# Attention scores as four column tiles of 32 keys with staged queries, in a two-layer conv, scan, attention and expert kernel

## What is computed

```python
qkv = jnp.einsum('bnc,ce->bne', x, W_qkv)          # B=4, N=4096, C=128
q, k, v = jnp.split(qkv, 3, axis=-1)               # HEADS=4, DIM_HEAD=32
q = l2norm_axis1(q); k = l2norm_axis1(k)           # over the tokens
sim = jnp.einsum('bihd,bjhd->bhij', q, k) * SCALE
attn = jax.nn.softmax(sim, axis=-1)
out = jnp.einsum('bhij,bjhd->bhid', attn, v)
```

## Time and profile before

| | |
|---|---|
| three runs | 6005.42, 6006.07, 6010.80 us; median 6006.07 |
| profiled execution | 5990.85 us, its span 5989.1 us |
| TensorE matmul busy | 4802.9 us (80%) |
| VectorE busy | 5104.7 us (85%) |
| ScalarE busy | 3730.3 us (62%) |
| attention loops | four stretches; the first begins at 822 us and its last exponential starts at 1384 us |

### The profile page before, as it was taken

How to read it: one execution, slowest core, us unless ns; L and a number is a source line. 1 busy time by engine, 2 the same in 40 slices (tenths; PEclk the granted TensorE clock), 3 DMA queues, 4 the chain that set the end, 5 groups by cost and what they waited for, 6 DMA issues and landing times. The chain is left out here.

```text
span 5989.1 us, 76415 instructions
## 1 busy us (share of the span) xinstructions
PE 4802.9 (80%) x21528; PEld 1760.4 (29%) x21592; DVE 5104.7 (85%) x6562; ACT 3730.3 (62%) x4769; POOL 1754.4 (29%) x1306
## 2 busy tenths in 40 slices
PE   5767779998666777999867677799986767789997
PEld 2222422223322242222332224222233222422223
DVE  6799779998779977999868996799987899679998
ACT  1666368883266636888326663788832666378882
POOL 3488500000148850000014885000001588400000
PEclk8899989999889998999988999899988899989998
DMA  1000020000000002000000000200000000020000
GB/s 38 0 1 0 15 54 0 0 0 22 22 0 1 0 15 54 0 0 0 22 22 0 1 0 15 54 0 0 0 22 22 0 1 0 15 54 0 0 0 15
DMA packets 26646, 69.25 MB, mean 12 GB/s; under 512 B 11224, under 2 KB 13088, under 8 KB 23328
## 3 DMA queue, kind: packets, MB, share of 16 engines
q1 hardware_dynamic: 26400, 66.43, 4.4%
HBM read 26.55 MB, written 8.39 MB: 6 GB/s over the span
## 5 line engine op out<-in xcount | busy, mean ns | idle before, releaser
L1257 ACT ACTIVATE arena<-ps 128x1024 f32<-128x1024 f32 x2048 | 1982.8, 1024 | 282.7 <-PE ps L1228 242.0
L1272 DVE TENSOR_TENSOR arena<-arena 128x1024 f32<-128x1024 f32 x1664 | 1913.9, 1220 | 130.3 <-ACT arena L1257 130.2
L916 DVE TENSOR_TENSOR_SCAN arena<-ps,hlast,arena 128x512 f32<-128x512 f32 x1024 | 1267.3, 1281 | 5.2 <-DVE arena L898 3.2
L876 POOL TENSOR_TENSOR arena<-arena 128x1024 f32<-128x1024 f32 x512 | 1206.9, 2357 | 22.6
L1228 PE MATMUL ps<-arena 128*128 (+1 forms) x4096 | 1079.8, 384 | 87.5 <-issue 61.6
L1212 PE MATMUL ps<-arena 128*32 128x512 f32 x8192 | 1077.0, 603 | 38.2 <-DVE arena L1277 35.2
L845 ACT ACTIVATE ps<-arena,amat 128x512 f32<-128x512 f32 x1024 | 692.0, 688 | 508.2 <-DVE arena L916 507.5
L813 PE MATMUL ps<-arena,ident 128*128 128x512 f32 x2048 | 970.2, 597 | 7.7 <-POOL arena L876 7.7
L1572 POOL MEMSET arena<- 128x1024 f32 x4 | 3.8, 956 | 2771.8 <-POOLq L101 2771.8
L1228 PEld LDWEIGHTS ps<-arena 128*128 128x128 f16 x4096 | 316.1, 98 | 1194.6 <-ACT arena L1257 807.1
L898 DVE TENSOR_TENSOR arena<-arena,ps 128x1024 f32<-128x1024 f32 x512 | 618.4, 1208 | 45.2 <-remote 30.9
(11 more groups left out here) (242 smaller groups left out, 4402.5 us busy)
## 6 DMA issues: line engine op xcount, KB each, us to landing
arena<-x SPq DMA_DIRECT2D x32, 512.0 KB, 5.9
arena<-arena SPq DMA_DIRECT2D x64, 256.0 KB, 6.0
arena<-arena SPq DMA_DIRECT2D x64, 224.0 KB, 5.8
arena<-pe SPq DMA_DIRECT2D x256, 32.0 KB, 1.8
out<-arena SPq DMA_DIRECT2D x8, 1024.0 KB, 3.9
expw<-L_ffn_expert_w SPq DMA_DIRECT2D x1, 512.0 KB
wqkv<-L_attn_W_qkv SPq DMA_DIRECT2D x1, 192.0 KB
wx<-in_projT SPq DMA_DIRECT2D x1, 128.0 KB
```

The source lines that it names most:

```text
L876: pool.tensor_tensor(halves(g[s % 4]), halves(hb[s % 4]), cs[s % 4].unsqueeze(1).broadcast_to([128, HD, CH]), ALU.mult).then_inc(hc_s, 1)
L916: dve.tensor_tensor_scan(halves(hb[s % 4])[:, h, :], da(s, h), halves(dbx[s % 2])[:, h, :], k.hlast[:, s, h, :], ALU.mult, ALU.add).then_i ...
L1257: act.activation(probs[p % 8], k.bank(2 * group[p], 2 * CH), ACT.Exp, scale=SCALE / SPLIT ** 2).then_inc(exp_s, 1)
L1272: dve.tensor_tensor(acc[p % 2], acc[p % 2], probs[p % 8], ALU.add).then_inc(acc_s, 1)
```

## The change

Each score matmul of 128 keys becomes four of 32 keys, each in its own column tile of the array (as the weighing has it), with the same 512 moving queries. The queries of a chunk are first copied by SP into one of two fixed buffers (at QL_AT, where the low part of the queries is no longer needed), one for even and one for odd chunks, so that all addresses are fixed. SP copies chunk c when the scores of chunk c-2 are done. The loop over chunks 1 to 7 becomes a loop of three turns with two chunks each, and a last chunk behind it; so there are four copies of the chunk's code instead of two.

```diff
+def staged_queries(k):
+    return [k.at(QL_AT + i * 2 * CH, 2 * CH).bitcast(F16).rearrange("p (h n) -> p h n", h=HEADS) for i in range(2)]
...
                     for e in range(2):
                         h = 2 * a + e
-                        last = pe.matmul(k.bank(2 * group[p] + e), ks[:, h, j * 128:(j + 1) * 128],
-                                         qs[:, h, cols_of(c)], start=True, stop=True)
+                        for t in range(4):
+                            last = pe.matmul(k.ps[32 * t:32 * t + 32, (2 * group[p] + e) * CH:(2 * group[p] + e + 1) * CH],
+                                             ks[:, h, j * 128 + 32 * t:j * 128 + 32 * t + 32], queries[:, h, :],
+                                             start=True, stop=True, tile_position=(0, 32 * t))
                     last.then_inc(s_mm, 1)
...
-        body(0, True)
-        pe.wait_ge(k.sem("q_rest"), 4 * HEADS * 16)
-        with pe.Fori(1, NCH) as c:
-            body(c, False)
+        def staged(c, i, n):
+            pe.wait_ge(staged_s[i], n * 16)
+            body(c, q_now[i], False)
+
+        body(0, qs[:, :, 0:CH], True)
+        with pe.Fori(0, NCH // 2 - 1) as cc:
+            staged(cc * 2 + 1, 1, cc + 1)
+            staged(cc * 2 + 2, 0, cc + 1)
+        staged(NCH - 1, 1, NCH // 2)
...
             sp.wait_ge(k.sem("q_rest"), 4 * HEADS * 16)
+            staged_s = [k.sem("q_even_staged"), k.sem("q_odd_staged")]
+            qs = k.at(QS_AT, 2 * L).bitcast(F16).rearrange("p (h n) -> p h n", h=HEADS)
+            for c in range(1, NCH):
+                if c >= 3:
+                    sp.wait_ge(k.sem("scores_mm"), (c - 1) * 2 * (L // 128))
+                sp.dma_start(staged_queries(k)[c % 2], qs[:, :, cols_of(c)]).then_inc(staged_s[c % 2], 16)
+            for i in range(2):
+                sp.wait_ge(staged_s[i], 16 * ((NCH - 1 + i) // 2))
```

More of the change, by code:

```diff
@@ L1170, in qkv @@
     k.clear()
+def staged_queries(k):
+    return [k.at(QL_AT + i * 2 * CH, 2 * CH).bitcast(F16).rearrange("p (h n) -> p h n", h=HEADS) for i in range(2)]
 def attend(k):
     qs, ks = (k.at(a, 2 * L).bitcast(F16).rearrange("p (h n) -> p h n", h=HEADS) for a in (QS_AT, KS_AT))
+    q_now, staged_s = staged_queries(k), [k.sem("q_even_staged"), k.sem("q_odd_staged")]
     v, ao = k.at(V_AT, L), k.at(TNT_AT, L)
@@ L1219, in finish, with body @@
             ones_by(acc, False, True).then_inc(l_mm, 1)
-        def body(c, first):
+        def body(c, queries, first):
             for j in range(NJ):
```

## The result

The changed kernel takes 5905.05 us (median of four, 5899.19 to 5915.02) against 6008.43 for the kernel before: ratio 0.983, 95% interval 0.9813 to 0.9847. It is faster by 103 us; 99 had been forecast (6006 to 5907).

What follows compares the result with a forecast made beforehand. TensorE bounds attention, with VectorE 8% and ScalarE 12% behind. 124 gained, less 18 for missed branches and 7 for the clock, is 99: 5892 for the profiled execution, 5907 as median; range 5870 to 5965.

Steps and rivals of the forecast that it cites:

- The drain between tile shapes: In a plain key tile on TensorE, 1.73 of 1.96 is streaming; 0.23 is lost at two changes of shape.
- (1): Each score matmul as four at 128x32: a float16 wave of four takes 0.22, a plain tile 1.73.
- rival A: Slower: float16 score waves of four take 0.43, a tile 2.58 against 1.96, 611 in all, time 6600; chance 0.10.
- B: Issue becomes TensorE's bound: 0.08 per load and matmul, 24 pairs a tile 1.92, time 5990; chance 0.07.
- C: The drain comes with a change of operand or type and stays; only branches are paid: 6031; chance 0.05.
- (2): ScalarE's wait cycle: plain tiles ScalarE-bound at 1.84, 0.86 idle at sum tiles; E10 to E63 takes 53.1, gain 3.2.
- E10: Exponential 10 of a chunk on ScalarE; forecast to start 12.49 after the end of the previous chunk's E63, before 13.17.
- E63: Exponential 63 of a chunk on ScalarE, its last; forecast to end 66.6 after the end of the previous chunk's.
- (3): Head of a chunk, from the end of E63 to E10: 12.49 instead of 13.17 without drains, gain 0.7.
- First chunk, 3.7: The first chunk of a batch, with no chunk before it to finish, gains 3.7 where the others gain 3.9.
- (4): Price of longer code: TensorE misses at eight back edges, 2.3 each, sum 18; clock falls book 7 more.
- (5): SP's query copies, 4 KB a partition per chunk, cost nothing; without the cover, a landing time of 7 us per chunk.

Runs made afterwards that it cites:

- written-out run: The changed kernel with its loop over chunks written out, so no back branch in attention; measured 0.9841 of the kernel before.

## Why the prediction was right, step by step

- *The drain between tile shapes, 0.23 a tile.* Right, and shown from three sides: 0.86 and 0.86 after, though float16 and float32 still take turns; 0.97 with fixed addresses at 128x128; 0.98 and 1.00 with tiles of 64.
- *(1) A float16 wave takes 0.22.* Right (1.05 for sixteen). Rivals A (0.43 a wave) and B (0.08 for a load with its matmul, measured 0.055) fall with it; C falls with the 0.86 of the point before. The 81 ns that B took from the Trainium skill ("TensorE: Matmul & The Clock Gate", Back-to-back issue gap) are given for matmuls of 128 moving columns; these move 512, four tiles at a time, so the 0.055 doesn't test them.
- *(2) The ring, 53.1 from E10 to E63.* Measured 53.05 (E10 12.50, E63 65.55 after E0). ScalarE idles 0.86 at a sum tile, and the sixth sum tile cost 0.73 where 0.86 was computed. The sign "ScalarE idle for about 4.6 us of a 66.6 us chunk" did not come: it is 6.7 (66.45 - 59.76). The forecast kept ScalarE's busy time at 61.98; exponentials that follow each other without a gap overlap, and it fell to 59.76.
- *(3) The head, gain 0.7.* From the end of E63 to E10 12.39 was measured where 12.49 was forecast; before it was 13.18, so the gain is 0.8. Per chunk 4.06 against 3.9; all undisturbed chunks together 128 against 124. "VectorE keeps pace and has no slack to give": right on the mean, but its eight buffers let single chunks run ahead of it, which I left out.
- *First chunk, 3.7.* The jump's second cost was missing. With the code moved it is 64.25, a gain of 3.9; in the changed kernel TensorE stops for 2.5 to 3.4 in each of the four first chunks, which lose 14 to a late instruction page. This is the one term that was absent from the sum.
- *(4) Eight missed branches, 18, and the clock, 7.* The misses came where they were forecast, 3.3 to 3.9 instead of 4.3; ScalarE's gap grew by 2.1 to 3.0. The chunks around the eight cost 28 against 25, but the split was wrong. In four such pairs of chunks no clock fell (one in the repeated changed kernel, three with the moved code); a miss alone costs 1.6 to 2.0 there, not 2.3, so about 15 for eight. The other 13 are eight falls of the clock at 1.5 to 1.7, where I had booked half a fall each as a consequence of the miss: only five of them come behind the branch, three come at the head of the chunk before it, some 60 us earlier. That 18 + 7 lies near 15 + 13 is luck.
- *The page's 2,048 instructions* (the Trainium skill, "Runtime: NRT & Kernel Launch", Instruction fetch mechanics): it pointed the right way, but as a limit for a loop it is too high here; 1,863 instructions missed, 1,701 did not.
- *(5) Staging costs nothing.* Right: 0.08 a chunk gained with staging alone. With one buffer its cover is gone and a chunk takes 68.5; the price of a missing cover was forecast too high, at 7 a chunk, where the scores waited 2.55.
- *Two slips that change nothing.* At 200 instructions to a page 3,264 are 16 pages, not 15 (the written-out run shows 257 to a page, so 13); and rival A, with the 25 for the branches, is 6642 rather than 6600.

So in attention 99 were forecast and 86.4 found: 14 for the late page and 3 more around the branches, less 4 for chunks that gained more than computed. That the medians differ by 103, close to the 99 of the forecast, is in part luck: 17 of it, more than the term that I missed, isn't found in the attention of the profiled executions, and on the second chip the difference is 94.

## What to carry to other kernels

Where matmuls of two kinds alternate on TensorE, give both the same tile shape: a change of shape costs 0.1 us each time here, even when each side is dense. Count the instructions when a loop body grows: splitting matmuls may make the loop larger than what TensorE holds of its code, and the place at which a far jump lands matters too. When an engine is no longer the bound, walk the ring of waits with its latencies before adding work or taking it off; here one more pair of lookahead was worth 42 us, and a sixth sum tile cost 19 without it and gained 26 with it.

## What the runs showed of the hardware

- A change of tile shape costs TensorE 0.11 to 0.14 (0.97 to 1.00 where 0.86 is streamed; up to 0.02 of it is the load of the stationary operand), between 128x128 and 128x32 as between 128x64 and 128x32.
- Column tiles of 128x32 in float16 take 0.22 for four, so 0.055 for a load with its matmul, with fixed addresses.
- A loop of 1,701 TensorE instructions stays where it is (branch 0.21), one of 1,863 doesn't (3.3 to 4.0).
- After a far jump TensorE stopped a second time, for 2.5 to 3.4, at the next 16 KB of code; moving the code by 80 instructions removed the stop, and the kernel before and staging alone have none.
- The granted clock falls to its lower level at chunk heads where TensorE's longest pause shortly before was 1.25 to 1.45, and each fall costs a 66 us chunk 1.5 to 1.7.
